# A graph layer with residual and layer norm on one Trainium2 core: one-column closing matmuls, zero matmuls beside the means, layer 1's first sum ahead of two means, and layer 2's products in another order

## The reference, cut to what matters

```python
sums   = segment_sum(edge_attr, src, 6250)          # 100,000 edges x 64 features
counts = segment_sum(ones, src, 6250)
mean   = sums / maximum(counts, 1)
combined = concat([x, mean, u expanded], axis=1)    # 6250 x (256 + 64 + 128)
h   = relu(combined @ W1 + b1)                      # 6250 x 512
y   = h @ W2 + b2                                   # 6250 x 256
out = layernorm(x + y)                              # over the 256 columns
```

## Time and profile before

| | |
|---|---|
| median of 3 runs | 831.62 us (831.08 to 832.5) |
| the profiled execution | 830.44 us, its span 828.5 us |
| mean granted TensorE clock | 0.988 |
| busy: PE, PEld, DVE, ACT, POOL | 92%, 86%, 86%, 65%, 49% of the span |
| end of the table's matmuls (949) | 699.82 us |
| z of step 0, step 2, step 24 | 716.17, 725.43, 822.03 us |

### The profile page before, as it was taken

The page is one execution under the profiler, slowest core; times in us unless marked ns, Lnnn a source line. Parts: engine busy times, 40 slices in busy tenths (PEclk is TensorE's granted clock), DMA queues, the critical chain, the costliest instruction groups (busy, mean ns, idle before and its releaser), DMA issues. The chain is left out here.

```text
span 828.5 us, 31441 instructions
## 1 busy us (share of the span) xinstructions
PE 763.8 (92%) x11398; PEld 715.1 (86%) x11399; DVE 711.5 (86%) x2317; ACT 539.7 (65%) x1128; POOL 402.8 (49%) x410
## 2 busy tenths in 40 slices
PE   9889999999989989998989978999999998899995
PEld 4689888888879888888888878999999997899995
DVE  8999999899988977987888707999999997799995
ACT  1356655666656646555656557888888885588886
POOL 3066666667666666656666660000000001598994
PEclk9999999999999999999999999999999999899999
DMA  6355555556656555555556448888888889711111
GB/s 206 130 193 195 197 188 195 201 179 203 200 182 202 184 187 184 190 187 185 189 187 181 161 151 278 267 262 260 265 262 258 265 259 242 171 53 61 63 62 63
DMA packets 74034, 156.37 MB, mean 189 GB/s; under 512 B 10851, under 2 KB 51044, under 8 KB 73239
## 3 DMA queue, kind: packets, MB, share of 16 engines
q1 hardware_dynamic: 57096, 102.33, 41.5%
q0 software_dynamic: 16896, 53.54, 17.2%
HBM read 95.47 MB, written 60.37 MB: 188 GB/s over the span
## 5 line engine op out<-in xcount | busy, mean ns | idle before, releaser
L604 POOL DMA_INDIRECT sorted_rows<-payload,idx x264 | 290.5, 1101 | 190.7 <-ACT payload L654 105.5
L867 PE MATMUL ps<-attr_buf,perm 128*128 128x198 bf16 x3168 | 308.8, 253 | 12.6 <-issue 8.4
L867 PEld LDWEIGHTS ps<-attr_buf,perm 128*128 128x128 bf16 x3168 | 287.8, 97 | 25.3 <-issue 18.7
L654 ACT CAST payload<-ps 128x792 bf16<-128x792 f32 x264 | 211.6, 832 | 146.0 <-PE ps L867 101.5
L1164 DVE TENSOR_SCALAR perm<-place_of,pos 128x512 bf16<-128x512 int16 x792 | 242.9, 365 | 23.3 <-PE ps L867 14.0
L1254 DVE TENSOR_SCALAR onehot<-node_of,sup 128x256 bf16<-128x256 int16 x838 | 183.3, 282 | 37.8 <-DMA sup<-sorted_rows 19.3
L949 PE MATMUL ps<-sup,onehot 128*128 128x64 bf16 (+1 forms) x6192 | 199.9, 193 | 5.2 <-issue 2.2
L949 PEld LDWEIGHTS ps<-sup,onehot 128*128 128x128 bf16 x6192 | 195.9, 97 | 9.2 <-issue 7.4
L624 POOL TENSOR_TENSOR xs<-xs,b_all 125x256 f32<-125x256 f32 x50 | 37.9, 782 | 203.8 <-DMA xs<-in_x 203.8
L722 ACT ACTIVATE apart<-node_of,sup 128x256 bf16<-128x256 int16 x194 | 96.6, 498 | 31.2 <-PE ps L949 30.2
L794 PE MATMUL ps<-xt,w1x 128*128 128x125 f32 x800 | 100.2, 279 | 2.9 <-ACT xt L659 2.5
(11 more groups left out here) (150 smaller groups left out, 606.8 us busy)
## 6 DMA issues: line engine op xcount, KB each, us to landing
sup<-sorted_rows SPq DMA_DIRECT2D x129, 396.0 KB, 4.0
attr_buf<-in_edge_attr SPq DMA_DIRECT2D x43, 576.0 KB
xs<-in_x SPq DMA_DIRECT2D x5, 1120.0 KB
out<-weights_z SPq DMA_DIRECT2D x25, 224.0 KB
x_stage<-in_x SPq DMA_DIRECT2D x47, 112.0 KB
sorted_rows<-payload,idx POOLq DMA_INDIRECT x264
pre<-jump_d SPq DMA_DIRECT2D x1, 1560.0 KB
pre<-first_d SPq DMA_DIRECT2D x1, 780.0 KB
```

Source lines behind the costliest of these rows:

```text
L604: pool.indirect_dma_start(out=sorted_rows, out_offset=bass.IndirectOffsetOnAxis(ap=idx[:, n:n + 1], axis=0), in_=payload[s][:, :], in_offs ...
L654: nc.scalar.copy(payload[s][:, :].rearrange("p (r w) -> p r w", w=PART), slots_p[s % PSUM_BUFS]).then_inc(s_pay, 1)
L867: last = nc.tensor.matmul(slot_p[s % PSUM_BUFS][r].rearrange("p (h f) -> p h f", f=PLANE), places, parts(a, t * CB + s), start=(t == 0 and ...
```

## The change

Four edits, all in the third stretch.

- The eight closing matmuls write one column in place of 455 or 260.
- Behind them TensorE waits for the second mean (`s_agg` 2, banks 6 and 7 read) and then runs 17 zero matmuls of 252 columns into the unused columns of bank 7. Nobody reads them.
- VectorE's order around the first sums: one split, two means, the other split, `hidden_sum(0, 0)`, two means, `hidden_sum(1, 1)`.
- Layer 2 of a step takes the 16 products with the high part for both columns first, then the 8 with the low part; the starting flag is set once per bank.

```diff
+UNUSED = 512 - (BUCKETS - (PAIR_BANKS - 1) * BANK_COLS) * ROW
+FILLERS = 17
...
+        unused_p = bank(BANKS - 1, UNUSED, 512 - UNUSED)
...
             for k in range(BANKS):
-                last = nc.tensor.matmul(table_p[k], zeros[:, :], zeros[:, 0:1].to_broadcast([P, table_p[k].shape[1]]),
-                                        start=False, stop=True)
+                last = nc.tensor.matmul(table_p[k][:, 0:1], zeros[:, :], zeros[:, 0:1], start=False, stop=True)
             last.then_inc(s_table, 1)
+            pe.wait_ge(s_agg, 2)
+            for k in range(FILLERS):
+                nc.tensor.matmul(unused_p, zeros[:, :], zeros[:, 0:1].to_broadcast([P, UNUSED]), start=True, stop=True)
...
-                for c in range(2):
-                    for part in range(2):
+                for part in range(2):
+                    for c in range(2):
                         if part == 1:
                             pe.wait_ge(s_h_lo, g * 2 + (c + 1 + 4))
...
-                                                        start=(part == k == w_part == 0), stop=(part == 1 and k == KH - 1))
+                                                        start=(c == part == k == w_part == 0),
+                                                        stop=(c == part == 1 and k == KH - 1))
...
             for k in (6, 7, 0, 1):
                 mean(k)
             dve.wait_ge(s_agg, 4)
-            for q in range(2):
-                split_means(q)
-            for k in (2, 3, 4, 5):
+            split_means(0)
+            for k in (2, 3):
                 mean(k)
+            split_means(1)
             hidden_sum(0, 0)
+            for k in (4, 5):
+                mean(k)
             hidden_sum(1, 1)
```

## The result

Of 20 runs of each kernel the median went from 832.07 us to 826.44 us. The ratio is 0.9954, with a 95% interval of 0.9931 to 0.9976, so 3.8 us less (2.0 to 5.7), faster by more than the 0.2% that can be told; the medians alone lie 5.6 us apart, within that interval. The ratio leaves out two runs of the changed kernel (833.4 and 833.96 us) that took over 1.5% more than its fastest. 3.7 us and a median of 827.9 were forecast. The profiled execution took 826.68 us, its span 824.8 against 828.5: 3.7 less as well. The runs scatter by several us either way, mostly ahead of the table, so one total says little about an edit worth 1 us. What follows is read from spans inside the third stretch of the profiles, from the record of the table's last matmul to z (VectorE's first reading of layer 2's result) of steps 0, 20 and 24.

The account below looks back on a forecast made before the run. The prediction took the chain of waits after the table as the bound, its steps a closed loop without slack. Start -2.8, steps 0 and end -0.9 gave -3.7 us: 830.44 to 826.7, median 827.9, range 824.3 to 830.0.

Parts of the forecast that it names:

- The closing: Eight closing matmuls after the table, one column each: 0.28 us in place of 1.40, 1.12 less.
- The zero matmuls: 17 matmuls ahead of step 0's transposes: 1.85 us at full clock, 3.7 at half; keeping the clock was called even.
- Rival 2: Zero matmuls don't keep the clock and hold the transposes until 705.7: start -1.1, end -0.9, 829.6 us; chance 0.15.
- Step 0: From the table's end to step 0's z: 3.45 us earlier with the clock, 2.1 if it falls half-way; 2.8 taken.
- the cover of layer 2: In step 0, the 16 high products (1.9 to 3.4 us) run within the 3.3 us of relu and GpSimd, hiding low clock.
- The steps: Ten pairs of steps after step 0 keep 8.66 us each, a gain of 0; odd z about 0.36 earlier.
- b at LB: LB is an even step's low-part start, b that step's z; b was forecast to stay at LB + 3.57 us.
- the lost races: VectorE's split cast comes up just as GpSimd starts its add: 0.60 us more, in three of ten splits between steps.
- Rival 1: The steps speed up too, the split slipping elsewhere between GpSimd's instructions: 2.2 us more, 825.7, or 824.3; chance 0.25.
- rival 3: The split loses to GpSimd each time in the steps: seven more at 0.6 us, +0.5 in all, 832.1; chance 0.05.
- The end: After step 20, without a split, low part to z falls from 3.56 to 3.1 us: twice 0.45, 0.9 less.
- The sum: Over the whole kernel, -2.8 and -0.9 give -3.7 us: 830.44 becomes 826.7, the median 831.62 becomes 827.9.

Follow-up runs that it names:

- additions behind the split: Changed kernel, with GpSimd's b2 additions after even steps 2 to 20 waiting for the split's second part: first span 12.88 us, steps 87.98, last span 17.19.
- the changed kernel again: The changed kernel, unaltered, rerun for 5 rounds on one chip against the kernel before: ratio 0.9965, median 782.89 us against 786.56.

## Why the prediction was right, step by step

*The closing.* Forecast -1.12, measured 1.40 to 0.19 in the chain, and 1.22 in the read. The first cast did wait for GpSimd's add, 0.41 in place of 0.29; the transposes came at 704.09 for a forecast of 704.2. (The floor of 0.1 each named there is over half, not a quarter, of the 0.175 that an old closing matmul took; nothing hangs on it.)

*The zero matmuls.* Forecast as even, and so it was. Of seven profiles with all 17, three kept the clock (2.03 us for the 17: after, additions behind the split, the changed kernel again) and four lost it (2.90 to 3.58). The Trainium skill (TensorE: Matmul & The Clock Gate, "What's actually happening") calls the activity check free-running, and the same 17 matmuls behind the same 2.04 us of pause came out both ways, as that would give. Without them TensorE's pause was 3.9 us and the clock fell in all four profiles; with eight it fell in both. What they are worth is then not the 1.0 us of the pair (12.98 against 14.00): when the clock is lost, they stand in the queue at half speed and the first span is 14.1 to 14.5 (the last being 15.70 less the 1.22 of the old closing), 0.1 to 0.5 more than without them. By three of seven that is about 0.3 us on the average against none (14.00), and next to nothing against eight (13.75): an estimate, with one profile for each of the two. Rival 2 of the prediction (the fall among the zero matmuls) is therefore no other kernel but four executions in seven, and the loss of it was over-priced: the transposes came 0.7 to 1.4 late, the 1.5 of the prediction being the worst case.

*Step 0.* Forecast 3.45 with the clock, 2.1 when it falls half-way, 2.8 taken. Measured in z of step 0: 3.28 by the profiles' own zero, 3.37 from the table's end, with the clock; 1.9 to 2.2 without. Of the 3.37, 1.22 lie ahead of VectorE's first read, 0.77 between the transposes and the first sum (2.90 to 2.13) and 1.50 behind it (8.17 to 6.67); between the first read and the transposes 0.12 were lost. The step that was right for a reason I had wrong is the cover of layer 2. I held that a low clock there would be hidden behind relu and GpSimd. In the ten profiles with the new order the way from the first sum to z of step 0 took 6.62 to 6.69 us, and in all ten the granted clock was 1.00 from the first matmul of that layer 2 to z: there was no low clock to hide. In the three with the old order it took 6.83, 8.17 and 8.30, and in the latter two the clock fell to half there. Whether TensorE's longer unbroken run at that place is why the clock stays up can't be settled by these runs.

*The steps.* Forecast 0, measured -0.03. The mechanism named holds in the changed kernel: b at LB + 3.51 (forecast 3.57), with the add gone 3.39, and the lost races gone too. In the kernel before it was TensorE's old order that ended the leg at 3.57; the split alone would have ended it at 3.51. The row that the prediction leaned on (765.70 to 769.26) could not tell the two apart, since the old order gives 3.57 with and without the add. The closeness of -0.03 is luck. It is a sum of two: six pairs shorter by 0.04 to 0.08, and a fourth lost race, at the short split of 799.62 (0.84 us), for 0.4. With three lost races, as before, the steps took 87.72 (old closing, eight zero matmuls), 0.57 less. The odd z came 0.11 earlier for a forecast of 0.36, with TensorE as what it waited for (734.76): that is the leg's 3.38 in place of 3.15 to 3.2, of which more under the end. The Trainium skill (SBUF — State Buffer, "Who interferes with whom") has an exclusive lock in which one of the two is blocked for the other's whole instruction. The trace agrees but for 0.14 us: the split's second part takes 0.84 us with the add and 0.43 without, and ends 0.29 behind the add (739.10 to 739.39), not 0.43. Rival 1 is refuted in its reason (the split doesn't slip elsewhere), rival 3 too: lost races were 1 to 4 in the nine profiles that have the adds where they were, not ten.

*The end.* This is the term that was mis-sized. I had -0.9 (twice 0.45); measured -0.41. A first part of the miss lay in the prediction itself, which took the leg as 3.1 here and as 3.15 to 3.2 in the steps, where the same sum gives 0.36 to 0.41 each. The rest is the four low products: they don't take 0.136 each but 0.74 in all, since the last one's own length stands at the end: low part to z is 3.36, not 3.1. Against that stands what no term had: the old order leaves 16 matmuls on the path of the last step, and in two of its three profiles the clock was low there, 18.74 and 18.98 against the 17.57 of the third; the ten with the new order have 17.16 to 17.21. The profile shown before was the better case.

*The sum.* -2.8 and -0.9 against -3.37 and -0.41 in the profiles, -3.8 in the runs by their ratio. The agreement is closer than the parts deserve: the start was under-sized in the profiled execution by its luck with the clock, and the end over-sized.

## What to carry to other kernels

Find out how a loop of several engines closes: write its legs as durations, add them, and see which of two ends of a leg will be left when one goes; an order that saved 0.2 us a leg on TensorE gave 0.08, since VectorE's split beside GpSimd's add ended the same leg. Filler matmuls in a queue are a wager: eight that are done in time even at half clock held nothing back, 17 that only fit at full clock cost up to 0.5 us in four of seven executions. And put the work that needs only the early half of an input ahead of all that waits for the late half, so that the last wait is followed by the least work.

## What had not been expected of the hardware

One chip ran the kernel before in 786.56 us (16 runs), against 832.07 in the 20 runs of the result. The difference lies ahead of the table: the table's first matmuls start at 452.41 in the kernel with layer 2's order alone on that chip, and at 496.18 in the profile before, while the last span of the new order is 17.16 to 17.21 on all chips. The experiments' other chips gave 835.34 and 787.38 in one run each. Which is the usual time, and why the sort is slower on some, stays open.
